# A transformer-like layer on one core: slot scores made transposed by one product per half, natural exponentials by transposes

## What is computed

```python
s = hs @ Ws1.T @ Ws2.T + bs2                      # rank 16 between the two
s = jnp.clip(s, -CLAMP, CLAMP).reshape(B, T, H, M).transpose(0, 2, 1, 3)
z = jax.lax.cumlogsumexp(s, axis=2)
es = jnp.exp(s)
enz = jnp.exp(-z)
A = jnp.where(mask, jnp.einsum('bhtd,bhjd->bhtj', q, k) * scale, 0.0)
ok = enz * jnp.einsum('bhtj,bhjm->bhtm', A, es)
qv = jax.nn.softmax(ok, axis=-1)
W2 = jnp.where(mask, jnp.einsum('bhtm,bhjm->bhtj', qv * enz, es), 0.0)
o = jnp.einsum('bhtj,bhjd->bhtd', W2, v)
```

## Time and profile before

| | |
|---|---|
| median of 3 runs | 822.07 us (820.96 to 822.13) |
| the profiled execution, its time | 823.12 us |
| the profiled execution, span | 821.3 us |
| mean granted TensorE clock | 0.976 |
| PE busy | 777.2 us (95%) |
| PEld busy | 660.5 us (80%) |
| DVE busy | 582.5 us (71%) |
| ACT busy | 435.3 us (53%) |
| POOL busy | 285.7 us (35%) |
| chain that ended last | PE 90%, DVE 6%, POOL 1%, ACT 1% |

### The profile page before, as it was taken

One profiled execution on the slowest core, in us unless ns is written; L12 is line 12 of the kernel. 1 busy time (PEld: TensorE's weight loads), 2 busy tenths in 40 slices (PEclk: granted clock), 3 DMA queues, 4 the chain that ended last, 5 costly groups with the idle time before them and its releaser, 6 DMA issues.

```text
span 821.3 us, 14494 instructions
## 1 busy us (share of the span) xinstructions
PE 777.2 (95%) x4571; PEld 660.5 (80%) x4571; DVE 582.5 (71%) x1502; ACT 435.3 (53%) x1188; POOL 285.7 (35%) x291
## 2 busy tenths in 40 slices
PE   7899999999999995799999999999999999999963
PEld 6788888888888884478888888888888888888852
DVE  4555545555555557869887988798888788887786
ACT  3455565555556542465656466556564665555420
POOL 6221010201101014435536346355364463563222
PEclk8999999999999998899999999999999999999997
DMA  7110101101010100100101001001001010000001
GB/s 229 36 52 6 46 13 38 49 2 51 13 38 13 51 1 14 53 1 13 53 0 38 25 13 51 0 13 51 0 20 44 13 51 0 13 0 0 1 1 52
DMA packets 23654, 23.76 MB, mean 29 GB/s; under 512 B 2369, under 2 KB 23361, under 8 KB 23506
## 3 DMA queue, kind: packets, MB, share of 16 engines
q1 hardware_dynamic: 23090, 22.98, 8.9%
q10 hardware_dynamic: 544, 0.52, 0.2%
HBM read 22.45 MB, written 1.05 MB: 29 GB/s over the span
## 4 chain that ended last, share of the span: by engine, by line
PE 90%; DVE 6%; POOL 1%; ACT 1%; issue 1%; DMA 0%; DVEq 0%; ACTq 0%; POOLq 0%
PE ps L1277 22%; PE ps L1493 11%; PE ps L1386 7%; PE ps L1284 5%; PE ps L1307 5%; PE ps L1505 3%; PE ps L1350 3%; PE ps L1391 3%; PE ps L1326 3%; PE ps L1530 3%; PE ps L1517 2%; PE ps L1547 2%; PE ps L1549 2%; PE ps L1548 2%; PE ps L1506 2%; PE ps L1519 2%
## 5 line engine op out<-in xcount | busy, mean ns | idle before, releaser
L1277 PE MATMUL ps<-xT_hi,w_hi 128*128 128x512 f32 x256 | 110.4, 431 | 3.9 <-DVE rot L1013 3.6
L1277 PE MATMUL ps<-xT_hi,w_lo 128*128 128x512 f32 x256 | 102.0, 398 | 0.0
L1277 PE MATMUL ps<-xT_lo,w_hi 128*128 128x512 f32 x256 | 101.5, 397 | 0.0
L1043 DVE TENSOR_TENSOR wt<-ps,const 128x384 f32<-128x384 f32 x128 | 68.3, 555 | 41.7 <-PE ps L1506 21.9
L383 POOL TENSOR_TENSOR w_lo<-w_raw,w_hi 128x512 fp32r<-128x512 f32 x32 | 40.8, 1286 | 155.7 <-ACT w_hi L536 155.7
L438 POOL TENSOR_TENSOR rot_s<-rot_s,const 128x512 f32<-128x512 f32 x64 | 82.0, 1293 | 21.2 <-ACT rot_s L679 21.2
L581 ACT ACTIVATE wt<-wt,negmax 128x128 f32<-128x128 f32 (+1 forms) x128 | 56.6, 443 | 28.1 <-DVE negmax L907 28.1
L895 DVE TENSOR_TENSOR v<-ps,bv_b 128x256 f32<-128x256 f32 x64 | 27.1, 423 | 51.8 <-PE ps L1284 51.8
L698 ACT ACTIVATE v<-ps 128x256 f32<-128x256 f32 x64 | 24.5, 382 | 72.6 <-PE ps L1493 72.3
L1032 DVE RECIPROCAL enz<-zs 128x128 f32<-128x128 f32 x64 | 60.4, 944 | 1.0 <-ACT zs L685 1.0
L1277 PEld LDWEIGHTS ps<-xT_hi,w_hi 128*128 128x128 f32 x256 | 49.2, 192 | 13.3 <-issue 4.5
(11 more groups left out here) (172 smaller groups left out, 2252.3 us busy)
## 6 DMA issues: line engine op xcount, KB each, us to landing
w_raw<-a_w_q SPq DMA_DIRECT2D x8, 256.0 KB, 2.6
wv<-a_w_v SPq DMA_DIRECT2D x8, 256.0 KB, 3.5
wo<-a_w_o SPq DMA_DIRECT2D x8, 256.0 KB, 2.7
w_raw<-b_Wq SPq DMA_DIRECT2D x8, 256.0 KB, 2.6
w_raw<-b_Wk SPq DMA_DIRECT2D x8, 256.0 KB, 3.3
wc<-b_Wv SPq DMA_DIRECT2D x8, 256.0 KB, 3.5
wc<-b_Wg SPq DMA_DIRECT2D x8, 256.0 KB, 3.7
wo<-b_Wo SPq DMA_DIRECT2D x8, 256.0 KB, 2.6
```

Of the source, the lines that this page charges most:

```text
L1043: d.tensor_tensor(dst, src[:, 0:384], tri3, ALU.mult).then_inc(done, 1)
L1277: ins = mm(PJ[n[0]], w[:, m, c, h * P:(h + 1) * P], x[:, c, cols], start=(t == 0), stop=(t == len(terms) - 1))
```

## The change

The score product is turned over: the slot weights of the pair (a float32r copy of 96 rows, `ws2p`) are stationary and the 512 tokens of the half stream through once, so the scores arrive transposed and their exponential is esT at once. The 96 rows are three groups of 32 (high and low parts of the slot rows and of the weights), built once: wider s1 products, a ScalarE copy and a VectorE subtraction (`s1_tail`) per batch row, and a cast and subtraction of ws2 before phase A's loop. es and es_hi now come from four transposes (et), which move to z's place in the even block; z moves behind the output product, two tasks on. GpSimd's `exp_tail` moves behind two rope products, and GpSimd copies the pair's weights (`pair_slots`) in block b=1. VectorE's reciprocals shift by one: 0 and 1 in the odd block, 1 ahead of the ok scaling; 2 and 3 in the next even block.

```diff
...
-B_TASKS = ["s", "q0", "q1", "z", "k0", "k1", "c0", "c1", "c2", "et", "c3"]
+B_TASKS = ["s", "q0", "q1", "et", "k0", "z", "k1", "c0", "c1", "c2", "c3"]
...
-        s1 = sb("s1", [P, B * T])
...
+        ws1x = sb("ws1x", [P, C, S_ROWS])
+        s1_one = sb("s1_one", [P, 1])
+        s1s = sb("s1s", [P, B * T], F32R)
+        ws2s = sb("ws2s", [P, HEADS * M], F32R)
+        ws2p = sb("ws2p", [P, P], F32R)
...
+        ws2 = enz[:, :, :].rearrange("p t m -> p (t m)")
...
-            sp.wait_ge(init_done, 3)
-            sp.dma_start(ws2[0:RANK, :], b_ws2).then_inc(small_ld, 16)
-            sp.dma_start(ws2[BIAS_ROW:BIAS_ROW + 1, :], b_bs2.rearrange("(o n) -> o n", o=1)).then_inc(small_ld, 16)
+            sp.wait_ge(init_done, 2)
+            for g in range(S_ROWS // S_GROUP):
+                sp.dma_start(ws2[g * S_GROUP:g * S_GROUP + RANK, :], b_ws2).then_inc(ws2_ld, 16)
+            for g in (0, 2):
+                row = g * S_GROUP + RANK
+                sp.dma_start(ws2[row:row + 1, :], b_bs2.rearrange("(o n) -> o n", o=1)).then_inc(ws2_ld, 16)
...
-            g.memset(s1[:, :], 0.0).then_inc(init_done, 1)
-            g.memset(ws2[:, :], 0.0).then_inc(init_done, 1)
+            g.memset(ws2[0:S_ROWS, :], 0.0).then_inc(init_done, 1)
+            g.memset(ws1x[:, :, :], 0.0).then_inc(ws1x_zero, 1)
...
+            pool.wait_ge(const_ld, 16)
+            g.tensor_tensor(s1_one[:, :], ident[:, RANK:RANK + 1], ident[:, 2 * S_GROUP + RANK:2 * S_GROUP + RANK + 1],
+                            ALU.add).then_inc(ws1x_done, 1)
+            pool.wait_ge(small_ld, 16 * 5)
+            pool.wait_ge(ws1x_zero, 1)
+            for r in range(S_ROWS // S_GROUP):
+                g.tensor_copy(ws1x[:, :, r * S_GROUP:r * S_GROUP + RANK], ws1[:, :, :]).then_inc(ws1x_done, 1)
...
-            def exp_tail(phase, half):
-
-                pool.wait_ge(b_es_hi, phase + 1)
+            def pair_slots(i):
+
+                g.tensor_copy(ws2p[0:S_ROWS, :], ws2s[0:S_ROWS, bass.ds(i * P, P)].bitcast(F32)).then_inc(b_ws2p, 1)
+
+            def exp_tail(n, phase, half):
+
+                pool.wait_ge(b_es, phase + 1)
+                pool.wait_ge(b_.proj_evac[n[0]], n[1])
...
                             split_tail(b_, i + 1, 2)
-                        if rest:
-                            exp_tail(phase, 1 - b // 2)
                         rms(x + b)
                         if rest:
                             rope_mul(n("q0"), 0, 0)
                             rope_mul(n("q1"), 0, 1)
+                            exp_tail(n("et"), phase, 1 - b // 2)
                         if nxt:
                             slots(x + b + 1, (b + 1) % B)
...
                             split_tail(b_, i + 1, 1)
+                            pool.wait_ge(b_.proj_ps, slot_ps(i, 1, 0))
+                            pair_slots(i + 1)
...
+            pool.wait_ge(ws2_done, 1)
+            pair_slots(0)
             pool.wait_ge(table_ld, 16)
-            exp_tail(0, 0)
             for j, (m, k) in enumerate(((0, 0), (0, 1), (1, 0), (1, 1))):
                 rope_mul(slot_done(0, 0, B_TASKS.index(ROPES[j])), m, k)
+                if j == 1:
+                    exp_tail(slot_done(0, 0, B_TASKS.index("et")), 0, 0)
                 if j >= 2:
...
+                act.wait_ge(ws1x_done, 1)
                 act.wait_ge(s1_ps, b + 1)
-                s.activation(s1[0:RANK, b * T:(b + 1) * T], ps[0:RANK, ffns[0].banks[b], 0:T], ACT.Copy).then_inc(s1_done, 1)
+                s.activation(s1s[0:S_ROWS, b * T:(b + 1) * T], ps[0:S_ROWS, ffns[0].banks[b], 0:T], ACT.Identity,
+                             bias=s1_one[0:S_ROWS, 0:1]).then_inc(s1_hi, 1)
...
-            act.wait_ge(small_ld, 16 * 7)
+            act.wait_ge(small_ld, 16 * 5)
             s.activation(w8b[:, :, :], w8[:, :, :].bitcast(I8), ACT.Copy).then_inc(cast_done, 1)
             s.activation(gwh[:, :], gw[:, :], ACT.Copy, scale=0.5).then_inc(gwh_done, 1)
+            act.wait_ge(ws2_ld, 16 * 5)
+            s.activation(ws2s[0:S_ROWS, :], ws2[0:S_ROWS, :], ACT.Copy).then_inc(ws2_hi, 1)
...
                 if name == "s":
 
                     act.wait_ge(b_.proj_evac[bank], count + 1)
-                    s.activation(es[:, tl, :], clip.rearrange("p (t m) -> p t m", t=HT), ACT.Exp).then_inc(b_es, 1)
-
-                    act.wait_ge(b_es, phase + 1)
-                    s.activation(es_hi[:, :].rearrange("p (t m) -> p t m", t=HT), es[:, tl, :], ACT.Copy).then_inc(b_es_hi, 1)
+                    s.activation(esT[:, half * HALF:(half + 1) * HALF], clip, ACT.Exp).then_inc(b_est, 1)
...
                 elif name == "et":
                     act.wait_ge(b_.proj_ps, done)
-                    s.activation(esT[:, half * HALF:(half + 1) * HALF], PJ[bank], ACT.Copy).then_inc(b_.proj_evac[bank], 1)
+                    s.activation(es[:, tl, :], PJ[bank].rearrange("p (t m) -> p t m", t=HT), ACT.Copy).then_inc(b_es, 1)
+                    s.activation(es_hi[:, :], PJ[bank], ACT.Copy).then_inc(b_.proj_evac[bank], 1)
...
                         if rest:
                             t("q1")
-                            t("z")
+                            t("et")
...
+                        if rest:
+                            t("z")
                         act.wait_ge(b_qt_ps, x + b + 1)
...
@@ -777,12 +807,9 @@
                             s.activation(oT, src, ACT.Copy).then_inc(b_.oT, 1)
                         else:
                             s.activation(oT_hi[:, b // 2, :, (b % 2) * T:(b % 2 + 1) * T], src, ACT.Copy).then_inc(b_.o_hi, 1)
-                        if rest:
-                            t("et")
...
-            act.wait_ge(init_done, 3)
...
-                if name == "et":
                     b_okexp_step(0)
...
+            def s1_tail(b):
+
+                rows, cols = slice(S_GROUP, 2 * S_GROUP), slice(b * T, (b + 1) * T)
+                dve.wait_ge(s1_hi, b + 1)
+                d.tensor_tensor(s1s[rows, cols], ps[rows, ffns[0].banks[b], 0:T], s1s[rows, cols].bitcast(F32),
+                                ALU.subtract).then_inc(s1_done, 1)
...
+            low = slice(2 * S_GROUP, S_ROWS)
+            dve.wait_ge(ws2_hi, 1)
+            d.tensor_tensor(ws2s[low, :], ws2[low, :], ws2s[low, :].bitcast(F32), ALU.subtract).then_inc(ws2_done, 1)
...
-            ffn_quant(0, 2)
+            ffn_range(0, 2)
+            s1_tail(0)
+            s1_tail(1)
+            ffn_round(0, 2)
             ln_scale(1, 3)
             ffn_quant(0, 3)
...
-                        b_recip(None, b // 2, 3)
+                        b_recip(None, b // 2, 2)
                         if rest:
                             b_rope_cos(n(1), 0, 0)
...
                         if rest:
                             b_rope_cos(n(2), 1, 0)
-                            b_recip(n(3), half, 0)
+                        b_recip(None, b // 2, 3)
+                        if rest:
                             b_rope_add(4 * phase + 1, 0, 0, half)
...
-                            b_gate(n(6), phase, 0, half)
-                            b_recip(None, half, 1)
+                            b_gate(n(7), phase, 0, half)
+                            b_recip(n(5), half, 0)
...
                         if rest:
-                            b_gate(n(7), phase, 1, half)
+                            b_gate(n(8), phase, 1, half)
                         if last and b == 3:
                             ffn_out(1, 0)
                         b_gated(x + b, b)
                         if rest:
-                            b_gate(n(8), phase, 2, half)
+                            b_gate(n(9), phase, 2, half)
+                            b_recip(None, half, 1)
                         if nxt:
                             b_okn_max(x + b + 1, (b + 1) % B, 2 * i + (b + 1) // 2)
...
                             ffn_range(1, 2)
-                        if rest:
-                            b_recip(None, half, 2)
                         (add_y if last else add_group)(b_, x + b, b)
...
-            b_recip(n0(3), 0, 0)
             b_rope_add(1, 0, 0, 0)
...
-            b_rope_cos(n0(5), 1, 1)
-            b_recip(None, 0, 1)
+            b_recip(n0(5), 0, 0)
+            b_rope_cos(n0(6), 1, 1)
             b_rope_add(4, 1, 1, 0)
             ln_scale(2, 3)
-            b_gate(n0(6), 0, 0, 0)
+            b_gate(n0(7), 0, 0, 0)
+            b_recip(None, 0, 1)
             tail(1, 2, ffns[0].banks[2])
-            b_gate(n0(7), 0, 1, 0)
+            b_gate(n0(8), 0, 1, 0)
             b_scores(0)
...
             b_slots(0)
-            b_recip(None, 0, 2)
+            s1_tail(2)
+            s1_tail(3)
...
-                    ins = mm(ps[0:RANK, ffns[0].banks[b], 0:T], ws1[:, c, :], xT[:, c, b * T:(b + 1) * T],
+                    ins = mm(ps[0:S_ROWS, ffns[0].banks[b], 0:T], ws1x[:, c, :], xT[:, c, b * T:(b + 1) * T],
...
+            pe.wait_ge(ws1x_done, 4)
             s1_product(0)
             s1_product(1)
```

(23 more changed lines are left out.)

16 lines of the change are left out of this document (7 added, 9 removed).

## The result

The changed kernel takes 855.78 us (median of 4 runs, 851.59 to 856.94), the kernel before 821.52 (4 runs, 817.59 to 822.13): ratio 1.0418, 95% interval 1.0369 to 1.0468. The profiled run took 856.94 us with a span of 855.1 (before: 823.12 and 821.3), so the two traces differ by 33.8 us. One execution of experiment 8 (992.66 us) and one of the kernel before (1548.62 us) lie far above all others of their kernels and stand in no ratio.

What follows compares the result with a forecast made beforehand. TensorE, busy 59.92 of 60 us in steady phase B, was taken as the bound, so its waits count. Terms 7.5 + 7.6 - 0.3 + 2.1 + 5.3 + 0.9 = 23.1 on 822.07 gave 845.2 us; 80% range 831 to 857.

Steps and rivals of the forecast that it cites:

- the four new waits: TensorE in the loop: W2 for zT, ok product for the masks, last output matmuls for oT_lo, "s" for GpSimd's copy.
- The score product: Even block's start: eight records become one product, but W2 waits for zT; 0.07 of 0.66 us saved per set.
- faster: Rival: TensorE's 99.9% taken at its word, zT ready earlier, 0.66 us per set counts; 817 or 812 us, chance 0.05.
- Even block: Score product -0.07, z behind the output product +0.70, qp wait -0.13: +0.50 per set, 15 times, +7.5 us.
- The pair's copy: GpSimd's slot-weight copy in block b=1 delays "s" and W2: +0.3 us, seven times, +2.1 (0 to 5).
- Odd block: Reciprocal 1 ahead of the ok scaling delays oT_lo and the last two output matmuls: +0.54 us, 14 times, +7.6.
- Between the phases: Slot-row subtractions delay rounding, the first slot copy and clip (+5.5), with smaller terms: +5.3 us, ends 2.0 and 7.5.
- four smaller terms: Between the phases: zs wait and reciprocal -1.9, lower-clock matmuls +0.7, z ahead of k1 +0.7, reciprocal 1 +0.9, "et" -0.6.
- Start and tail: Weight casts and copies before the first A loop 0 (ends 0 and 2); last pair's reciprocal 3 in the tail +0.9 us.
- The clock: Steady loop: granted clock taken as 1.00 despite new idle times of 0.9 and 0.7 us; falling clock, chance 0.12.
- Odd block covered: Rival: oT_lo is not late, because VectorE's order slides into the longer even block; 835.5 us, chance 0.13.
- only the ends cost: Rival: the loop cancels within itself, leaving +5.3 between the phases and +0.9 in the tail; 828 us, chance 0.07.

Runs made afterwards that it cites:

- experiment 8: The changed kernel without the running sum's two products of the exponentials' low part; 846.06 us, ratio 1.0293 to the kernel before.
- Experiment 3: The kernel before with only the first of the four products of the slot scores' task; 821.3 us, ratio 1.0004.
- experiment 4: The changed kernel with the new slot score product issued four times in a row, same scores; 857.73 us, ratio 1.044 to the kernel before.
- experiments 1 and 2: 1: changed kernel, reciprocals 0 and 1 earlier in the odd block, 836.99 us; 2: kernel before, reciprocals at the change's places, 834.5 us.
- Experiment 6: The changed kernel with GpSimd's first slot-weight copy put before its long wait between the phases; 848.56 us, ratio 1.0321 to the kernel before.
- Experiment 7: The changed kernel with GpSimd kept idle between the phases until VectorE's last two feed-forward adds are done; 851.22 us, ratio 1.0365 to the kernel before.
- the tenth experiment: The kernel before with z's copy first on ScalarE and the masks ahead of the clip on VectorE, in the even block; 823.7 us, ratio 1.0042.

## Why the prediction was right, and what it sized too small

The direction and the places of the four new waits came as predicted; 855.8 lies inside the range of 831 to 857, close to its end. The forecast of 845.2 added 23.1 us, the trace shows 33.8. Term by term:

**The score product**: 0.07 us was taken as saved per set, from the 1.26 of a block with b = 2 alone. Measured are 0.01 for b = 0 (1.36 and 1.35), and for b = 2 a W2 that starts 0.02 to 0.04 later. Experiment 3 shows that three products fewer are not felt, and experiment 4 the same for three more where b = 0. The rival "faster" is out by this.

**Even block**: +0.50 predicted, +0.67 measured. "z" costs its full 0.70 (experiment 8). The ok product kept its place. Too large was the wait for qp: 0.13 per set was taken off, while 0.70 less 0.67 leaves 0.03 for it and the score product together. Before the odd block's transposes the rows have 0.30 us from k1's last matmul (513.42 to 513.72), after the change 0.22: at this mark the wait cost 0.08, and the rest of the 0.13 belongs to the odd block. The pair's copy was taken at 0.3 in every second even block; those blocks are longer by 0.67 as the others are, so it cost about nothing by itself: the copy took 0.28, and "s" came 0.85 after the transposes, inside the wait for zT. Together the two terms were 9.6 and came to 9.7 (9.0 in the loop and 0.7 in the last pair). That they agree so well is partly luck, since the errors of the two cancel.

**Odd block**: the mechanism is shown by experiments 1 and 2. The size was 0.54, measured 0.76 to 0.80; 14 times 0.77 is 10.8 instead of 7.6. The last pair's odd block gained 0.17 instead of 0.3. The step that failed is "a reciprocal of 0.94, pipelined to 0.87, moves all behind it". The ok scaling stands 10.56 us behind the block's transposes and stood at 9.61 before, 0.95 more, since it starts 1.07 behind the reciprocal; so the two matmuls L1429 start 0.65 later and not 0.54. And from their start to the next transposes it is 1.28 us, against 1.13 before, though the matmuls between are the same: 0.15 more that the sum did not hold. PE's wait for oT_lo is 0.64 and not the 0.8 to 1.0 foretold, because another 0.26 us passes ahead of the first oT_hi matmul (514.03 to 514.52, ScalarE's copy ending at 514.37). This costs nothing more, as oT_lo comes later still.

**Between the phases**: +5.3 predicted, +11.5 measured, the largest error, and outside the stated end of 7.5. Up to the clip the chain came as written: +5.5 predicted, 6.3 measured, 0.3 of which came from phase A. Experiment 6 shows that GpSimd's late copy alone was worth 5.0. The step that failed is the list of "four smaller terms" behind the clip. With their signs they add up to -0.2, and this stretch grew by 5.3, from 26.26 us to 31.52. The list took 1.9 off for the reciprocal, which did come, and counted VectorE's other instructions at the durations of before. But the shift brought two-operand instructions beside GpSimd's products: 2.1 us more for the adds, 0.9 for the rope sum, 0.7 for the addition ahead of them (L907, 1.41 instead of 0.69). Experiment 7 takes 2.6 us of it back.

The other part of the rows is TensorE's lower clock. After 5.22 us without a matmul the six projection matmuls ahead of the second quantized product start 0.43 us apart (0.23 at a granted clock of 1.00; from 340 to 344 us it is 0.50), the product itself takes 1.06, and VectorE waits 2.35 us for it, where it had waited 0.18: its output comes 1.5 us later behind the clip. From the running sum's product to the first even block there are 1.9 us more; 1.4 of them are this product itself, now ahead of k1; it starts after 4.78 us without a matmul, and the granted clock from 354 to 358 us is 0.50. No run was made for this part alone, but experiment 4 bears on it. There the three additional score products stand ahead of the clip, the granted clock is 0.50 up to 344 us and 0.97 from 344 to 345, where the second quantized product starts (344.18) and takes 0.61, VectorE waits 1.81, only one of the two adds meets a GpSimd product (2.36 for both), and from the clip to the first even block it is 29.00 us instead of 31.52. So the two causes are not independent.

**Start and tail**: the start cost nothing that can be seen. The mark moved by 0.26, and the same row lies between 315.5 and 321.1 in the four traces with the code of before, and between 314.1 and 320.1 in the eight of the changed one. The tail is 2.1 longer between these two traces instead of 0.9, but this says nothing: from the last even block to the end it is 42.6 us before and 44.6 in experiment 3, with the same code there, and 43.1 in experiment 6 against 44.6 in the changed kernel, whose tails are the same too. Whether the reciprocal costs 0.9 stays open.

**The clock**: PE idled 0.64 us in each odd block, and in each even block 0.73 (b = 0) or 0.47 (b = 2) and once more 0.21, 5% of the stage in all, and the granted clock stayed 1.00 from 380 to 780 us, as the sum had taken it. No trace shows a clock that falls in the loop, the case that had the chance of 0.12 and, in a partial form, a place in the range: from 380 to 780 us it is 1.00 in all twelve. The tail of before, with 0.50 from 783 to 786 us behind idle times of 0.81 and 1.11, did not carry over to it.

**Odd block covered** and **only the ends cost** fall too: both blocks grew by as much in every set. "PE busy at some 93%" was low; it is 95%, and a pair is 2.9 us longer, not 2.4. That the total still came inside the range rests on the range's width: in the traces the sum missed by 10.7 us, the two large errors (6.2 between the phases, 3.2 in the odd block) having the same sign.

## What to carry to other kernels

An engine that is busy 99.9% of a stage may be filling a wait with work: before a product is made cheaper, find what the instruction behind it waits for, and whether that is ready at the new, earlier time. When a step is moved on an engine that is not the bound, look at what stands behind the new place and who waits for it; one reciprocal of 0.94 us too many ahead of a subtraction cost 0.8 us fourteen times. A task that is taken away can also have covered a second wait, as "et" did with the oT_hi copy. Behind a shifted chain, check also which two engines now work at the same time that did not before.

## What the runs showed of the hardware

VectorE's adds of two operands in SBUF, 128 x 512 fp32 (L1174 before, L1211 after), took 0.68 us each with GpSimd idle and 1.75 each beside GpSimd's tensor products. The rope sum took 1.55 in the changed kernel and 1.65 in experiment 7, both beside such a product, instead of 0.63 to 0.69, and in the loop of the changed kernel 1.14 beside es_lo (499.44). GpSimd's own subtraction es_lo took 1.73 between the phases of the changed kernel instead of 1.26 in experiment 7, as it already did at 337.52 in the trace before (1.74). In the changed kernel the rope sum ends at 350.54, 0.55 behind the end of GpSimd's product, and es_lo at 351.67, 1.13 behind the rope sum. Two of VectorE's operations with one operand in PSUM kept their time: in the tenth experiment oT_lo and the addition behind it took 0.68 each from 488.18 to 489.46, while GpSimd ran two products from 487.76 to 489.74. What the two engines meet at is not shown; the rows show the lengths alone.

Behind a wait of 0.64 us for oT_lo the same matmuls took 0.15 us more than in a running stream (1.28 against 1.13). The weight load of the first one starts together with its product there (both at 516.32), and 0.22 us ahead of it in an even block (501.00 and 501.22). In the loop of the changed kernel, with idle times of 0.21 to 0.73 us, three per set, the granted clock was 1.00 from 380 to 780 us. Between the phases it was 0.50 around the first matmuls behind 5.22 and 4.78 us without one (340 to 344 and 354 to 358 us).
